# A routed mixture of experts: the part before the first tile in another order, without unread products

## The reference

```python
h = h_norm * gamma[:, None, :] + beta[:, None, :]
probs = softmax(h_flat @ router_w); gates, idx = top_k(probs, 2); gates = gates / gates.sum(-1)
hid = relu(einsum('nd,edf->nef', h_flat, exp_w1) + exp_b1)
y = einsum('ned,ne->nd', einsum('nef,efd->ned', hid, exp_w2) + exp_b2, combine)
return x + y.reshape(x.shape)
```

## Time and profile before

| | |
|---|---|
| profiled execution, its own time | 495.7 us |
| its span, first to last instruction | 493.6 us |
| median of three runs | 494.72 us (493.55 to 495.49) |
| mean granted TensorE clock | 0.965 |
| busy share of the span | TensorE 94%, VectorE 78%, ScalarE 56%, GpSimd 45% |

### The profile page before, as it was taken

The page is one execution under the profiler, slowest core; times in us unless marked ns, Lnnn a source line. Parts: engine busy times, 40 slices in busy tenths (PEclk is TensorE's granted clock), DMA queues, the critical chain, the costliest instruction groups (busy, mean ns, idle before and its releaser), DMA issues.

```text
span 493.6 us, 15842 instructions
## 1 busy us (share of the span) xinstructions
PE 463.4 (94%) x5700; PEld 418.1 (85%) x5700; DVE 384.0 (78%) x1439; ACT 277.9 (56%) x838; POOL 224.4 (45%) x189
## 2 busy tenths in 40 slices
PE   7899768999999999999999999999999999999990
PEld 5754448899999999999999999999899999999990
DVE  4898778899888878878888888888888877777640
ACT  2467526566565566555566665566556555555440
POOL 0643221555454455554554454454555444444422
PEclk8789958999999999999999999999999999999997
DMA  8943673344444434434444443444444332322321
GB/s 315 407 143 129 214 180 130 81 101 112 91 88 92 95 87 90 119 87 89 98 89 91 113 92 88 93 93 93 109 96 88 53 49 46 55 45 46 53 26 21
DMA packets 37819, 51.67 MB, mean 105 GB/s; under 512 B 8064, under 2 KB 29840, under 8 KB 37488
## 3 DMA queue, kind: packets, MB, share of 16 engines
q0 software_dynamic: 13632, 18.91, 22.5%
q1 hardware_dynamic: 21488, 31.14, 19.5%
q10 hardware_dynamic: 2624, 0.62, 0.6%
HBM read 36.74 MB, written 18.11 MB: 111 GB/s over the span
## 4 chain that ended last, share of the span: by engine, by line
PE 80%; DVE 8%; DMA 5%; ACT 3%; issue 2%; POOL 1%; SPq 0%; ACTq 0%; DVEq 0%; POOLq 0%
PE bank L687 37%; PE bank L694 34%; PE bank L642 3%; DMA out_rows<-yout,tok 3%; PE bank L636 2%; PE bank L506 1%; DVE tns L784 1%; DMA par<-in_params 1%; PE bank L515 1%; ACT hid L461 1%; DVE bns L760 1%; DMA hg<-h_rows,tok 1%; DVE hidlo L1084 1%; DVE wlo L1069 0%; POOL whi L287 0%
## 5 line engine op out<-in xcount | busy, mean ns | idle before, releaser
L461 ACT ACTIVATE hid<-bank,par 128x128 f32<-128x128 f32 x568 | 162.2, 368 | 164.7 <-PE bank L687 162.9
L687 PE MATMUL bank<-hThi,whi 128*128 128x128 f16 x1136 | 189.4, 220 | 5.2 <-DVE hTlo L1074 1.6
L687 PE MATMUL bank<-hTlo,whi 128*128 128x128 f16 x1136 | 189.3, 220 | 0.0
L331 POOL DMA_INDIRECT out_rows<-yout,tok x71 | 119.6, 1684 | 110.5 <-ACT yout L473 85.7
L687 PE MATMUL bank<-hThi,wlo 128*128 128x128 f16 x1136 | 157.1, 220 | 0.0
L694 PE MATMUL bank<-whi,hidlo 128*128 (+1 forms) x568 | 154.8, 273 | 0.0
L694 PE MATMUL bank<-whi,hidhi 128*128 (+1 forms) x568 | 154.8, 273 | 0.0
L694 PE MATMUL bank<-wlo,hidhi 128*128 (+1 forms) x568 | 154.8, 273 | 0.0
L323 POOL DMA_INDIRECT hg<-h_rows,tok x71 | 83.5, 1176 | 112.7 <-DVE tok L1060 102.2
L687 PEld LDWEIGHTS bank<-hThi,whi 128*128 (+1 forms) x1136 | 111.6, 99 | 14.8 <-issue 7.1
L687 PEld LDWEIGHTS bank<-hTlo,whi 128*128 (+1 forms) x1136 | 111.9, 98 | 5.5
(11 more groups left out here) (170 smaller groups left out, 458.2 us busy)
## 6 DMA issues: line engine op xcount, KB each, us to landing
stage<-in_exp_w SPq DMA_DIRECT2D x64, 256.0 KB
whi<-in_x SPq DMA_DIRECT2D x8, 512.0 KB, 8.4
out_rows<-in_x SPq DMA_DIRECT2D x8, 512.0 KB, 16.1
h_rows<-wlo SPq DMA_DIRECT2D x8, 512.0 KB, 3.7
hg<-h_rows,tok POOLq DMA_INDIRECT x71
out_rows<-yout,tok POOLq DMA_INDIRECT x71
b2row<-in_exp_b SPq DMA_DIRECT2D x1, 1024.0 KB, 20.6
par<-in_params SPq DMA_DIRECT2D x1, 517.5 KB, 6.2
```

The costliest lines, as they stand in the source:

```text
L331: gp.indirect_dma_start(out=out, out_offset=bass.IndirectOffsetOnAxis(ap=tok[:, t:t + 1], axis=0), in_=yout[:, t % 2, :], in_offset=None, ...
L461: ins = S(hid32[:, par, c * P:(c + 1) * P], bk_hid[half][:, (c - 4 * half) * P:(c - 4 * half + 1) * P], ACT.Relu, bias=vcol[:, bass.ds(e * ...
L687: hid_ins = MM(o, lhs[w, k], h[:, par, k * P:(k + 1) * P], start=(n == 0), stop=(n == 3 * KD - 1))
```

## The change

All of it is in the first part.

- All calls of `warm` from the transposes of batch 0 to the first tile are taken out. Those before (24 at the start and 3 between the steps of the style chain) stay.
- TensorE's order: logits are issued for batches 0 to 3 together, then 4 and 5, then 6 and 7, with the batches in the inner loop, so that neighbouring instructions use different columns of the array. Transposes use six banks in place of five. `back` uses one bank up to its ninth half and two from then on; the two halves of batch 7 go between the prefix products after the selection.
- ScalarE's order follows: `deviation(1)` before the two table loads of the softplus, `deviation(2)` and `deviation(3)` earlier, the table of the square root and that of exp fetched ahead by a small instruction each. It no longer modulates batch 7; VectorE does (`modulate`). The router's exp also takes the second largest logit.
- VectorE's order: statistics of later batches stand earlier, one product of a pair (`g` times `gam`) is taken once for all, and the two selections are cut into steps, with the first one's last steps between the second one's. The sum of the two chosen exponentials is now 1 plus the exponential of the second, so GpSimd's chain of five steps becomes two, one of them ahead of the selection. `selh` is written with its tokens contiguous.
- SyncE stores the gates of batches 0 to 3 ahead of the rows of batches 6 and 7.

```diff
-        bk_T = banks[0:5]
-        bk_back = (banks[7], banks[5])
-        bk_log = (banks[6], banks[1])
+        bk_T = banks[0:6]
+        bk_log = (banks[6], banks[4])
+        def bk_back(i):
+            return banks[5] if i >= BP * 2 and i % 2 == 1 else banks[7]
...
+                gp.tensor_tensor(exr3, ex3, m8[:, 5, j0:j1].unsqueeze(2).broadcast_to([P, n, E]), ALU.mult).then_inc(s_gp, 1)
+                gp.wait_ge(s_gp, part + 1)
                 gp.wait_ge(s_sel, part + 1)
...
+                gp.tensor_tensor(comb3, exr3, chosen3, ALU.mult).then_inc(s_comb, 1)
...
+            deviation(1)
             act.wait_ge(s_sty_v, 1)
             S(sp[:, 1, :], sp[:, 0, :], ACT.Exp).then_inc(s_exp1, 1)
             act.wait_ge(s_u1, 1)
             S(sp[:, 3, :], sp[:, 2, :], ACT.Ln).then_inc(s_ln1, 1)
-            deviation(1)
+            nc.scalar.activation(junk[:, 0:2], cst[:, C_EPS:C_EPS + 2], ACT.Sqrt)
...
+            deviation(2)
             time_deviation(0)
             modulate(0)
-            deviation(2)
             modulate(1)
+            deviation(3)
+            half_rows(0, 0)
+            half_rows(0, 1)
             time_deviation(1)
-            half_rows(0, 0)
+            half_rows(1, 0)
             modulate(2)
             modulate(3)
...
+            def logits(b0, b1):
+                pe.wait_ge(s_h2, min(2 * b1, 14))
+                if b1 == B:
+                    pe.wait_ge(s_h2v, KD)
                 for k in range(KD):
+                    for b in range(b0, b1):
+                        i = b % BP
+                        ins = MM(bk_log[b // BP][EP * i:EP * i + EP, 0:T], rw[:, k * EP:(k + 1) * EP], hT[b][:, k * T:(k + 1) * T],
+                                 start=(k == 0), stop=(k == KD - 1), tile_position=(0, EP * i))
...
-            warm(18)
             pe.wait_ge(s_cst, 16)
             transposes(0, 0)
             transposes(0, 1)
-            warm(8)
             transposes(1, 0)
             transposes(1, 1)
-            warm(10)
             pe.wait_ge(s_sty_a, 8)
             transposes(2, 0)
-            warm(6)
             transposes(2, 1)
             transposes(3, 0)
             transposes(3, 1)
-            logits(0)
             transposes(4, 0)
-            back(0, 0)
-            logits(1)
-            back(0, 1)
             transposes(4, 1)
+            for g in range(2):
+                back(0, g)
+            back(1, 0)
             transposes(5, 0)
-            back(1, 0)
             transposes(5, 1)
-            logits(2)
             back(1, 1)
+            back(2, 0)
             transposes(6, 0)
-            logits(3)
             transposes(6, 1)
-            back(2, 0)
+            logits(0, BP)
             transposes(7, 0)
             transposes(7, 1)
+            logits_of_tokens(0)
             back(2, 1)
-            logits_of_tokens(0)
-            logits(4)
+            logits(4, 6)
             back(3, 0)
-            logits(5)
+            logits(6, 8)
             back(3, 1)
-            logits(6)
-            logits(7)
-            back(4, 0)
             logits_of_tokens(1)
...
+            back(7, 0)
             pe.wait_ge(s_ca, 1)
...
-            warm(10, 1)
+            back(7, 1)
...
-            warm(5, 1)
             slot_table(0, 0)
-            warm(6, 1)
             slot_table(1, 1)
-            warm(6, 1)
             slot_table(2, 0)
-            warm(6, 1)
...
+            def modulate(b):
+                ve.wait_ge(s_tr, 2 * b + 2)
+                ve.wait_ge(s_mc, b // 2 + 1)
+                for k in range(KD):
+                    at = b * KD + k
+                    V.tensor_scalar(hT[b][:, k * T:(k + 1) * T], bk_T[at % 6][:, :], hA[:, at:at + 1], hB[:, at:at + 1],
+                                    ALU.mult, ALU.add).then_inc(s_h2v, 1)
...
+                V.tensor_tensor(selh[:, :].rearrange("p (e j) -> p e j", e=E)[:, :, j0:j1], by_expert(tm, part), by_expert(oh1, part),
+                                ALU.add).then_inc(s_sel, 1)
```

More of the change, by code:

```diff
@@ L252, in _ @@
                 store_gates(sp_, b)
+            for b in range(6, B):
+                store_h(b)
             sp_.wait_ge(s_ord, 1)
@@ L432, in _ @@
             modulate(5)
-            half_rows(2, 0)
             time_deviation(3)
@@ new lines, in at_largest, with first_at, first_chosen @@
+            def at_largest(part):
+                ve.wait_ge(s_d, part + 1)
+                return mark(V.scalar_tensor_tensor(out=by_token(tm, part), in0=by_token(d1, part), scalar=0.0, in1=desc_b,
+                                                   op0=ALU.is_ge, op1=ALU.mult))
+            def first_at(i, a, part, done):
+                ve.wait_ge(s_v, done)
+                return mark(V.tensor_reduce(of_tokens(i, part), by_token(a, part), AX_X, ALU.max))
+            def first_chosen(part, done):
+                ve.wait_ge(s_v, done)
+                return mark(V.tensor_tensor(by_token(oh1, part), desc_b, over(1, part), ALU.is_equal))
@@ new lines, in others, with second_largest, at_second @@
+            def others(part, done):
+                ve.wait_ge(s_v, done)
+                return mark(V.scalar_tensor_tensor(out=by_token(d2, part), in0=by_token(oh1, part), scalar=-3e38,
+                                                   in1=by_token(d1, part), op0=ALU.mult, op1=ALU.add))
+            def second_largest(part, done):
+                ve.wait_ge(s_v, done)
+                V.tensor_reduce(of_tokens(2, part), by_token(d2, part), AX_X, ALU.max).then_inc(s_m2, 1)
+            def at_second(part):
+                ve.wait_ge(s_m2, part + 1)
+                return mark(V.tensor_tensor(by_token(tm, part), by_token(d2, part), over(2, part), ALU.is_ge))
@@ L866, in _, with two_sum, reciprocal @@
+            def two_sum(part):
+                ve.wait_ge(s_exp, part + 1)
+                return mark(V.tensor_scalar(of_tokens(4, part), of_tokens(4, part), 1.0, None, ALU.add))
+            def reciprocal(part, done):
+                ve.wait_ge(s_v, done)
+                V.reciprocal(of_tokens(5, part), of_tokens(4, part)).then_inc(s_rec, 1)
             ve.wait_ge(s_par, 16)
@@ L913, in _ @@
             ve.wait_ge(s_v, gam_done)
-            n = less_mean(0, n)
-            stats(5, 2, 3)
-            less_mean_gam(0, n)
+            V.tensor_tensor(pairs(gg[:, :]), pairs(gam[:, :]), g_k.unsqueeze(1).broadcast_to([P, B, KD]), ALU.mult)
+            n = less_mean_gam(0, less_mean(0, m))
             n = time_inverse(0)
-            last = stats(5, 3, 4)
-            shifts(0, scales(0, n))
-            moments(2, last)
+            stats(6, 2, 3)
+            n = scales(0, n)
+            stats(6, 3, 4)
@@ L945, in _ @@
             shifts(2, scales(2, time_inverse(2)))
[L946 to L949 removed]
+            time_stats(6, 0)
+            time_stats(6, 1)
+            time_stats(7, 0)
+            time_moments(3, time_stats(7, 1))
             less_mean_gam(3, less_mean(3, mean_of_h(3, mean_gained(3))))
[L951 to L953 removed]
+            a = largest(0)
+            n = scales(3, time_inverse(3))
+            less_largest(0, a)
+            shifts(3, n)
+            modulate(7)
+            a = first_at(1, tm, 0, at_largest(0))
+            a = others(0, first_chosen(0, a))
+            second_largest(0, a)
+            a = second_numbers(0, at_second(0))
+            b = largest(1)
+            a = first_at(3, d2, 0, a)
+            less_largest(1, b)
+            a = second_chosen(0, a)
+            b = at_largest(1)
+            both_chosen(0, a)
+            b = first_at(1, tm, 1, b)
+            a = two_sum(0)
+            b = first_chosen(1, b)
+            reciprocal(0, a)
+            b = others(1, b)
+            second_largest(1, b)
+            b = second_numbers(1, at_second(1))
+            b = first_at(3, d2, 1, b)
+            a = two_sum(1)
+            b = second_chosen(1, b)
+            reciprocal(1, a)
+            both_chosen(1, b)
             sel3 = selh[:, :].rearrange("p (e j) -> p e j", e=E)
```

222 lines of the change are left out of this document (107 added, 115 removed).

## The result

The changed kernel takes 497.76 us (median of eight executions, 495.91 to 499.22); the kernel before, timed beside it, 493.96 us (eight, 493.55 to 495.67). The ratio is 1.0064, 95% interval 1.0047 to 1.0081: it is slower by 0.64% (the two medians alone lie 3.8 us, or 0.77%, apart). The forecast was 496.2 us, no change on the slow side. The profiled execution took 499.22 us and has a span of 497.3 us; it is the longest of its eight, so sizes read from it are rather large.

What follows compares the result with a forecast made beforehand. The prediction took the chain of waits before the first product as what the change could move; 0.85 + 0.1 + 0.1 + 0.5 made 1.5 us later, 497.2 profiled, 496.2 us as median; own range 494 to 498.5, with rivals 491.5 to 500.5.

Steps and rivals of the forecast that it cites:

- The course of the clock: TensorE: half clock from 13 to about 42 us, at most short rises at 18 to 21 or 29 to 32.
- the first rival: At 41 to 47 us: clock stays low through logits of batches 0 to 3, +1.9 to +2.8, 498.7 us; chance 0.30.
- The logits: Batches 0 to 3 together on TensorE: 2.7 us at full clock, between 2.1 and 4.2.
- The four `shifts`: VectorE's add ending each pair of batches: second 2.2 us late, third level with before, fourth 3.2 late at 49.0.
- Selection: Second half, after the logits: starts 0.85 us later, keeps its 4.55 us length, last `selh` write shorter than 0.72.
- the sentence on the tail: After `selh`: gate stores start 0 to 0.5 us later, taken as 0.1; other stores land ahead of ScalarE's last.
- From gather to first product: Before the first tile: four small matmuls may run at the half clock, costing 0.1 us in the sum.
- The sum: Start of the first product: 0.85 + 0.1 + 0.1 + 0.5, 1.5 us later.
- The rival on the faster side: Clock up at about 29 us and stays, shortening round trips, transposes and logits: -4.2 us, 492.0; chance 0.24.
- The weighed rule: Transposes do not lift TensorE's clock as matmuls do, so it would rise only after the logits from 41.3 us.
- The reading behind the rise of the clock: TensorE's clock rises 3.4 to 5.3 us after unbroken work begins; from 38.7 that gives 42.1 to 44.0, taken as 42.9.
- the three rises: Clock rises in the trace before the change, read as 3.4, 5.2 and about 5 us after unbroken work began.

Runs made afterwards that it cites:

- the profile without late rows: Changed kernel, rows of batches 6 and 7 not stored, those of batches 0 and 1 stored a second time instead; 495.55 us, ratio 1.0023.

## Why the prediction was right or wrong

- **The course of the clock** came as forecast: half, with short rises near 20 and 31, and up late, from 44.62 to 61.7. The rise at 44.62 instead of 42.9 lay beyond the forecast's own 42.1 to 44.0. By its own sign (half at 44 us) the first rival had come in, but not its price: it took 5.4 us for the logits, and they took 3.24.
- **The logits** at full take 1.92 us, not the 2.7 chosen, and less than the lower end of 2.1. The two errors cancelled: fourth `shifts` at 49.10, forecast 49.0. That was luck.
- **The four `shifts`** were forecast at 25.2, 34.4, 40.0 and 49.0 and ended at 25.97, 34.60, 40.27 and 49.10. The first was 0.8 later than forecast, where VectorE's steps beside GpSimd took up to 0.42; the sum had 0.5 for that, which fits but was not tested.
- **Selection.** Start 54.19 (forecast 53.75), last write 0.34 us (0.29 to 0.72), its end 58.77 (about 58.5). GpSimd ran pair 1 right behind pair 0, sixteen blocks in 8.62 us from 12.57.
- **The failed step** is the sentence on the tail: stores 0 to 0.5 later, "taken as 0.1", and "both land ahead of ScalarE's last". The stores began 0.95 us sooner after `selh`, and the step measured +2.17 us in one profile and +1.57 in the other. It counted when a store is issued and which queue it is in, not how long it then takes to land. The last rows did land ahead of the last gates, but at 68.74, where they alone would have held the gather. In its place the runs show two costs, less the 0.95: some 1.4 us by which late rows put the landings off, and up to 1.6 us for a single late step. The cause of the second is open.
- **From gather to first product**, 0.1 for small matmuls became 0.35: the gather itself took 3.49 us in place of 3.15. No run tells why.
- **The sum** of 1.5 became 3.85 us in the profile and 3.8 between the medians; of the missing 2.3, 2.07 is the tail. The time lies within the forecast's own range of 494 to 498.5, but by its own mark of half a per cent (2.5 us) it is just beyond no change.
- **The rival on the faster side** (clock up at about 29 and staying, 492.0) is real in single executions: the profile without late rows is one, with the fourth `shifts` 4.1 us earlier, where the rival had worked out 4.2. For the changed kernel itself both profiles show the fall at 34.
- **The weighed rule.** From 14.88 to 41.92 us TensorE ran transposes alone, and the clock rose at 20.7 and 30.96. By the Trainium skill, "TensorE: Matmul & The Clock Gate", Part 4: PE-mode transpose, transposes would not engage it; this trace disagrees, for fp32 transposes written as here.

The reading behind the rise of the clock was wrong in one place. In the trace of the kernel before, the clock was not half up to 18.8 us; it was full until the slice from 8 (columns as in the earlier trace rows):

```profile
7.00:8.00 1.00, 0.10 (x2) 1.00 1.06 406
8.00:9.00 1.00, 1.00 (x7) 0.77 1.00 369
9.00:10.00 1.00, 1.00 (x7) 0.50 0.99 361
```

TensorE's list shows no gap there from 7.90 on, not only from 13.57, so the first of the three rises came 10.9 and not 5.2 us after unbroken work began. The narrow range for the rise did not follow from the rows.

Two things stay open. Why the same program has either course of the clock: the executions differ long before 20 us, and the first fall comes at 7.27, 9.39 and 10.48 us in the three profiles of this TensorE program. And what lengthens the tail: from `selh` to the gather it is 9.8 to 10.2 us in the eight profiles of the new order in which the clock stayed up through the alternation, whatever the order of the stores, but 10.85 to 11.45 in the four others. Those four have the 16 KB packet in the tail; of the eight only the one without late rows has it. No run parts the packet from the clock.

## What to carry to other kernels

Removing filler is free only as long as the work itself leaves no thin stretch: test the removal in the old order and in the new one, because here the new order with unread products cost nothing, the removal in the old order cost nothing, and the two together 3.8 us. When small stores end a critical path, ask what large transfers are in flight on every queue while they land and what else the next step waits for, not only where they stand in their own queue. And when times of a kernel spread more than those of the one before, read the spread before trusting one profile.

## What the runs showed of the hardware

- Four fp32 products in four groups of 32 columns ran in the time of one: sixteen instructions of 512 tokens in 1.92 us, four in 1.90, whether neighbours or batches alternate (1.94).
- The same TensorE program had the clock full from 29.9 to 60.6 us in one profile, and in two others up, down and up again.
- 16 KB gate stores ended 0.3 to 0.7 us apart alone, and beside 512 KB stores 2 us apart in one profile and 0.7 to 1.9 in the other.
- Fifteen of the sixteen steps of a 512 KB store were there at 67.22 us and the last at 68.74; a 16 KB packet of the instruction queue started at 65.64.
